# Graph layer kernel, first stage: half of the first-layer products earlier, sort steps on other slots

## The reference, cut to what matters

```
xn = layernorm(x)
Q = elu(xn @ Wq) + 1;  K = elu(xn @ Wk) + 1;  v = xn @ Wv
KV = sum over nodes of K^T v, per head;  Z = 1 / (Q . sum(K) + 1e-6)
msg = layernorm(((Q @ KV) * Z) @ Wm, g1, b1)
h = relu(concat(xn, msg) @ W1) @ W2
mix = xn + layernorm(h, g2, b2)
```

## Time and profile before

| | us |
|---|---|
| median of three runs (7422.92 to 7425.28) | 7423.68 |
| the profiled execution | 7417.52 |
| its span, first to last instruction | 7415.7 |
| projections | about 163 to 487 |
| slots | about 487 to 1190 |
| first instruction of the next stage on DVE (a clear of `acc`, L1063) | 1191.9 |

### The profile page before, as it was taken

How to read it: one execution, slowest core, us unless ns; L and a number is a source line. 1 busy time by engine, 2 the same in 40 slices (tenths; PEclk the granted TensorE clock), 3 DMA queues, 4 the chain that set the end, 5 groups by cost and what they waited for, 6 DMA issues and landing times. The chain is left out here.

```text
span 7415.7 us, 87393 instructions
## 1 busy us (share of the span) xinstructions
PE 5359.5 (72%) x25217; PEld 3726.8 (50%) x25217; DVE 5144.2 (69%) x11724; ACT 1896.7 (26%) x4599; POOL 3425.8 (46%) x3444
## 2 busy tenths in 40 slices
PE   5877774545455555551989978999899899984992
PEld 2446563333333443331664434444678787774661
DVE  6557776888888887777656767788666676664333
ACT  0333333222222332221414410011122222222220
POOL 0000003777777777770000056666677676755005
PEclk8998887777777777775989989999899999985996
DMA  2100002455455555552902332233333333343223
GB/s 87 41 27 1 1 1 68 126 123 125 123 124 127 132 132 130 130 128 50 274 19 122 133 105 84 83 87 90 86 98 97 95 99 93 95 108 108 64 64 120
DMA packets 368589, 704.52 MB, mean 95 GB/s; under 512 B 62713, under 2 KB 231946, under 8 KB 361099
## 3 DMA queue, kind: packets, MB, share of 16 engines
q0 software_dynamic: 164352, 455.61, 24.2%
q1 hardware_dynamic: 203765, 243.32, 9.9%
HBM read 546.83 MB, written 151.87 MB: 94 GB/s over the span
## 5 line engine op out<-in xcount | busy, mean ns | idle before, releaser
L2073 POOL DMA_INDIRECT ag_rows<-table,row_src x1612 | 1591.2, 987 | 1664.3 <-POOLq L2957 933.6
L1142 POOL DMA_INDIRECT at_rows<-table,row_dst x1612 | 1635.1, 1014 | 490.9 <-issue 449.2
L1308 PE MATMUL at_p_a<-at_rows,at_hot 128*125 128x264 f32 x3224 | 1135.3, 510 | 999.6 <-issue 979.0
L1308 PEld LDWEIGHTS at_p_a<-at_rows,at_hot 128*125 128x125 f32 x3224 | 707.4, 245 | 1186.9 <-issue 1047.5
L1271 DVE TENSOR_TENSOR acc<-acc,at_p_a 125x264 f32 x1612 | 687.0, 426 | 244.3 <-PE at_p_a L1308 101.1
L2183 DVE TENSOR_TENSOR mo_prod<-mo_far,mo_twice 125x256 f32<-125x256 f32 x1600 | 579.8, 418 | 51.2 <-issue 44.7
L2443 PE MATMUL mo_p_e<-ag_rows,ag_hot 128*125 128x256 f32 x1612 | 466.4, 414 | 145.5 <-DVE acc L2282 80.9
L1094 POOL PARTITION_ALL_REDUCE sb_top<-sb_top x1 | 0.4, 397 | 1200.6 <-DVE sb_top L1065 1200.6
L1258 DVE TENSOR_TENSOR at_rows<-at_rows 128x1024 f32<-128x1024 f32 x496 | 496.6, 1022 | 21.9 <-ACT at_rows L1190 21.7
L2282 DVE TENSOR_TENSOR acc<-acc,mo_p_e 125x256 f32 x806 | 336.7, 418 | 246.4 <-PE mo_p_e L2443 97.6
L2443 PE MATMUL mo_p_m<-ag_rows,ag_hot 128*125 128x256 f32 x1612 | 463.4, 412 | 40.2 <-DVE acc L2282 39.3
(11 more groups left out here) (516 smaller groups left out, 9792.6 us busy)
## 6 DMA issues: line engine op xcount, KB each, us to landing
at_wide<-node_t SPq DMA_DIRECT2D x124, 406.2 KB
moe_in<-ones SPq DMA_DIRECT2D x8, 6272.0 KB, 47.0
table<-rt_row SPq DMA_DIRECT2D x50, 1000.0 KB
at_rows<-table,row_dst POOLq DMA_INDIRECT x1612
ag_rows<-table,row_src POOLq DMA_INDIRECT x1612
acc<-moe_in SPq DMA_DIRECT2D x105, 128.0 KB, 2.1
moe_out<-acc SPq DMA_DIRECT2D x105, 128.0 KB, 1.7
table<-row SPq DMA_DIRECT2D x50, 128.9 KB
```

What stands on the lines that cost most here:

```text
L1142: pool.indirect_dma_start(out=rows[n % 3][:, g, :], out_offset=None, in_=m.table0, in_offset=bass.IndirectOffsetOnAxis(ap=row_i[:, n * G + ...
L1308: pe.matmul(p_a[k % BANKS][0:P, 0:TW], hot[n % 2][:, g, :], rows[n % 3][:, g, :], start=True, stop=True).then_inc(s_agg, 1)
L2073: pool.indirect_dma_start(out=rows[:, i % RING, j, :], out_offset=None, in_=m.table1, in_offset=bass.IndirectOffsetOnAxis(ap=row_i[:, 2 * ...
```

## The change

`early_plan` is written anew. Over the first 108 row pieces there are three sort steps to four row pieces (81 in all, 54 before), and in the slots a sort step follows slots 4, 5, 6 and 9 of each ten until all are placed, which is after slot 245. On PE the matmuls of W1's product that take xn are issued earlier: those of quarters 2 and 3 in slot 2, those of quarters 0 and 1 in slot 4, ahead of the wait for the normalized messages and behind the wait for the last layernorm of the pair before (`s_hn`). Only those that take the messages stay in slots 5 to 8. PE also waits once for W1's weights before the slots. On ACT the exponential moves behind the two relu copies of its slot; in slot 8 both exist.

```diff
--- before.py
+++ after.py
@@ -168,6 +168,7 @@
 SPAN = 10
 LEAD = 3
 TAIL = 6
+SORT_SLOTS = (4, 5, 6, 9)
 COUNTED = 2 + NT // MASKS + 2
 SORTED = len(LOCAL) * (len(LOCAL) + 1) // 2 + sum(1 + ph - 11 + 1 + 10 for ph in ACROSS) + 2
 
@@ -209,8 +210,15 @@
 
 def early_plan():
 
-    plan = ["sort"] * (2 * COUNTED) + ["rows", "rows", "sort"] * SORTED
-    return plan + ["rows"] * max(0, 6 + 2 * NT + 2 + LEAD + SPAN * PAIRS + TAIL + 1 - 2 * SORTED)
+    first_rows = 6 + 2 * NT + 2
+    plan = ["sort"] * (2 * COUNTED) + ["rows", "sort", "rows", "sort", "rows", "rows", "sort"] * (first_rows // 4)
+    left = SORTED - 3 * (first_rows // 4)
+    for slot in range(-LEAD, SPAN * PAIRS + TAIL):
+        plan.append("rows")
+        if slot % SPAN in SORT_SLOTS and left > 0:
+            plan.append("sort")
+            left -= 1
+    return plan + ["sort"] * left + ["rows"]
 
 
 def sorts_and_rows(nc, m, a, row_i, node_f):
@@ -788,12 +796,6 @@
                                 n = 2 * i + j
                                 act.activation(m.x[:, n, :], m.x[:, n, :], ACT.Identity, scale=rstd1[:, n:n + 1],
                                                bias=m.nmr[:, n:n + 1])
-                        i = pair_at(slot, -2)
-                        if i is not None:
-                            act.wait_ge(s_min, i + 1)
-                            if i >= 1:
-                                act.wait_ge(s_num, i)
-                            act.activation(qf[:, :, :], qmin[:, :, :], ACT.Exp).then_inc(s_exp, 1)
                         for half, p_h in enumerate((p_b, p_kv)):
                             i = pair_at(slot, 6 + 2 * half)
                             if i is not None:
@@ -802,6 +804,12 @@
                                     act.wait_ge(s_y, i)
                                 act.activation(ht[:, 2 * half:2 * half + 2, :].rearrange("p c n -> p (c n)"),
                                                p_h[:, 0:4 * P], ACT.Relu).then_inc(s_relu, 1)
+                        i = pair_at(slot, -2)
+                        if i is not None:
+                            act.wait_ge(s_min, i + 1)
+                            if i >= 1:
+                                act.wait_ge(s_num, i)
+                            act.activation(qf[:, :, :], qmin[:, :, :], ACT.Exp).then_inc(s_exp, 1)
                         yield
 
                 weave(plan, sort=sort_work(), rows=row_work())
@@ -899,7 +907,16 @@
                     yield
                     pe.wait_ge(s_sc, NT)
                     pe.wait_ge(s_wq, 32)
+                    pe.wait_ge(s_w1, 128)
                     pe.wait_ge(s_blocks, 1)
+                    def hidden(i, o, from_c):
+                        at = 2 * P * (o % 2)
+                        for c in (from_c, from_c + 1):
+                            moving = xnt[:, c, 2 * P * i:2 * P * i + 2 * P] if c < 2 else zt[:, c - 2, :]
+                            mm = pe.matmul((p_b, p_kv)[o // 2][:, at:at + 2 * P], w1[:, c, 128 * o:128 * o + 128], moving,
+                                           start=c == 0 and o % 2 == 0, stop=c == 3, skip_group_check=True)
+                        return mm
+
                     for slot in range(-LEAD, SPAN * PAIRS + TAIL):
                         i = pair_at(slot, 0)
                         if i is not None:
@@ -925,8 +942,16 @@
                                     mm = pe.matmul(p_a[0:P, C * j:C * j + C], mt[:, c, j, :], w_m[:, c, :],
                                                    start=c == 0, stop=c == 1)
                             mm.then_inc(s_o, 1)
+                        i = pair_at(slot, 2)
+                        if i is not None:
+                            for o in (2, 3):
+                                hidden(i, o, 0)
                         i = pair_at(slot, 4)
                         if i is not None:
+                            if i >= 1:
+                                pe.wait_ge(s_hn, i)
+                            for o in (0, 1):
+                                hidden(i, o, 0)
                             pe.wait_ge(s_xm, i + 1)
                             for c in range(2):
                                 for j in range(2):
@@ -937,14 +962,7 @@
                             i = pair_at(slot, 5 + o)
                             if i is not None:
                                 pe.wait_ge(s_zt, i + 1)
-                                if o == 0 and i >= 1:
-                                    pe.wait_ge(s_hn, i)
-                                p_h = (p_b, p_kv)[o // 2]
-                                at = 2 * P * (o % 2)
-                                for c in range(4):
-                                    moving = xnt[:, c, 2 * P * i:2 * P * i + 2 * P] if c < 2 else zt[:, c - 2, :]
-                                    mm = pe.matmul(p_h[:, at:at + 2 * P], w1[:, c, 128 * o:128 * o + 128], moving,
-                                                   start=c == 0, stop=c == 3)
+                                mm = hidden(i, o, 2)
                                 if o % 2 == 1:
                                     mm.then_inc(s_h, 1)
                         for j in range(2):
```

## The result

The changed kernel takes 7321.45 us in the median of four runs (7314.54 to 7324.34), beside 7423.3 us for the kernel before: a ratio of 0.9863, 95% interval 0.985 to 0.9875. The forecast was 7313 in a range of 7280 to 7375. The profiled execution has a span of 7312.8 us, 102.9 less than before.

A forecast was written before the change was run, and what follows sets the result against it. DVE's wait for Q's late product, with PE at half clock, was taken to bound the slots; -118.6 - 3.7 + 5.6 + 6.1 = -110.6 us gave 7306.9, with 6.2 for the median 7313, range 7280 to 7375.

The forecast's parts named there:

- The period: Slots, from one start of the denominators z to the next without a turn: 20.97 us in place of 26.86.
- The clock: PE in the slots: full clock, records at 0.21 us, slot clock above 0.95; half clock before cost about 3 us.
- Turns: Turns of the keys on PE, 12 left in the slots: 34 us in sum, bounds 0 and twice that.
- The projections: 27 sort steps moved there: those in the tiles cost 0, two among the statistics pieces +5.6 us, three turns +6.1.
- The head: Six statistics pieces, where PE waits for DVE: two moved sort steps, one plain, one with a flip, cost +5.6 us.
- the three turns: Projections, steps 67, 68 and 80, where PE is the bound: 1.9, 2.3 and 1.9, +6.1 us.
- The table load: ACT, now between relu and exponential: load 1.28 us, a switch costs 1.29; the move costs a period 0.1 us.
- signs of being wrong: Slots: periods over 23 us, DVE waiting over 2 us for ACT's exponential, kmin late in tiles without a turn.
- That rival: Table switch between relu and exponential costs double the row's 1.29 us: +31 us, 7344; chance 0.05.
- The clock rivals: PE's clock falls ahead of W1's messages part (period 23.9, 7382, chance 0.10) or stays at 1.2 GHz (7570, 0.03).
- The one for the projections: Rival: the moved sort steps aren't hidden in the projections, +61 us, 7374; chance 0.06.
- cross-check: Slots' period: one sort step less saves 2.43 us, gone idle time the rest, less 2.6 us of new waits.

The follow-up runs named there:

- the discarded products: Kernel before, with the early products issued and thrown away and all full products issued again behind them: 7357.56 us, ratio 0.9934.
- the kernel with slots 2, 4, 7 and 9: Changed kernel with a pair's four sort steps behind slots 2, 4, 7, 9 and the exponential ahead of the relu copies again: 7295.8 us, ratio 0.9841.

## Why the prediction was right

The forecast missed the median by 8 us of 102. Part of that closeness is luck: the stage itself was forecast 110.6 us shorter and is 96.5 shorter, a miss of 14.1, and 6.4 us of it were made up behind the stage, where the code is the same and the time is spread by 20 us. The mechanism held, though. By its steps:

- **The period.** 20.97 forecast, 21.08 to 21.09 measured in the periods without a turn, and every station within 0.16 us (table above). This is 24 x 0.11 = 2.6 us of the miss.
- **The clock.** "Before, the half clock cost about 3 us": 2.76 by the discarded products. The slots' clock was to be above 0.95 and is 0.95. The records were to take 0.21 us and take 0.22 (3.54 for 16). The clock isn't full, because records behind turns run at half clock, and because in three turnless periods (22.47, 22.42 and 22.41) and two with a turn PE still drops to 1.2 GHz, now at Wm's product, whose eight records take 2.94 to 3.43 us in place of 1.99:

```profile
725.64 3.16 PE L942 MATMUL rowbank<-mq_w_m,mq_mt 128*125 128x256 f32 x8 [0.67 <-ACT mq_mt L774]
```

- **Turns.** This term was mis-sized, and it is nearly all of the stage's miss: 34 us forecast, 47 measured above 24 x 21.08, 43 of them in periods with a turn. Behind slot 6 it was 5.8 to 7.3 us in place of 4.4 and 5.5, together 25.8 for 19.8; behind slot 5 7.4 for 6.7; behind slot 4 3.4 for 1.7; behind slot 9 6.3 for 5.7. Another 4.3 us lie in periods without a turn. The forecast's list of signs had 24 to 26 us for a turn behind slot 6, its own sum 25.4 to 26.5; 26.9 to 28.3 were measured. The step had turns wait and PE go on at full clock. The rows show PE's wait followed by records at half clock: 1.74 us for the quarter behind the turn at 595.13, where it is 1.01 at full clock, and 3.05 us for a turn at 759.75, where it is 1.97. In one of the four periods behind slot 6 (647.43 to 674.29) it is Wm's product instead, 2.94 us.
- **The projections.** "Those in the tiles cost 0" holds: tiles are at 6.41 with two steps in every second one. The head cost 5.5 for 5.6, the three turns 4.5 for 6.1.
- **The table load.** The relu at 832.41 took 0.59, the load came at 833.01, and the exponential at 834.31: 1.30 us from load to use, with the load on the path for the first time. One of the forecast's signs of being wrong did show beside a turn: DVE waits 2.7 us for the exponential in seven periods, six of them with a turn, and 0.7 to 1.1 in the other turnless ones. The new order was to cost a turnless period 0.1 us and gains it 0.2 (21.26 with the old one). The 1.38 us more of the Trainium skill, "ScalarE: Activation LUTs", section "What ACT_TABLE_LOAD costs", don't show. That rival is excluded by the row.
- **The rivals.** The clock rivals asked for periods of 23.9 and more without a turn; there are none. The one for the projections asked for late kmin; the tiles are at 6.41.

What the forecast had right in sum it had wrong in shares. Its cross-check put "the sort step less" at 2.43 of the 5.89 us of a period. The experiment with the early products alone shows 5.31 of the period's gain without any step less, and the stage ends 12 us earlier. On top of the early products the new plan with the old order on ACT loses 12.1 us (1083.1 to 1095.2): 5.4 in front of the first tile and 3.1 on to the first z, 7.3 in the periods, where turns and clock take more than the step brings, and 3.7 back at the end. The sum was right because it was made from a walk through the new period; the attribution was a story told beside it, and only undoing the parts could tell.

## What to carry to other kernels

When a chain leaves an engine idle in the middle of each period, products that don't need the late operand belong there, and their clock can be worth as much as their time: 2.76 and 2.55 us here. Once the wait is gone, walk through each part of a bundled change with the others in place, since a part that would have helped alone (the plan, 35 us alone) can lose on top of the rest. In a hand-written order, look at where a rare step that couples two engines (a turn) falls: one cost 5.8 to 7.3 us behind slot 6 in the changed kernel and 0.7 to 1.9 behind slot 4 in the kernel with slots 2, 4, 7 and 9; average counts per period don't show it.

## What the runs showed of the hardware that wasn't expected

- The length of a gap on PE doesn't settle the clock behind it. In the kernel with the exponential ahead, PE was idle 2.85 to 3.23 us ahead of W2's product in 16 periods; in eight the eight records behind took 1.99 us, in the other eight 2.55 to 3.57. The two longest gaps (3.20 and 3.23 us) were followed by full clock, one of 2.97 by 3.57 us.
- In the changed kernel, four transposes stand between two gaps ahead of Wm's product, the second of 0.67 us each time. Its eight records took 1.99 us in 20 periods and 2.94 to 3.43 in five. The second profile of that kernel has the same five (2.89 to 3.36) and one more (3.54), so it isn't all chance. Why in those is open.
- Issuing 200 matmuls more, with their results thrown away, made the kernel 51 us faster (ratio 0.9934): the three quarters took 5.17 us instead of 7.95, at a clock of 0.98 instead of 0.86.
- The switch of ACT's table cost 1.29 to 1.30 us from the start of the load to the start of the activation in 47 of the 48 switches of the changed kernel where the activation waited for nothing else, behind a copy and behind a relu (1.41 in the other).
